# A one-core language-model tower: a new order of the first stage's turn, masked CB kept in PSUM, interleaved chains, and list scatters two at a time

## The reference, cut to what matters

```
h = quantised_rows(table)[x]                       # abs-max per row, round to 127 steps
# SSD block, per sequence of 128 tokens
zxbcdt = layernorm(h) @ in_proj.T
xBC    = silu(causal_conv_4_taps(xBC) + conv_b)    # x (384), B (128), C (128)
dt     = softplus(dt_raw + dt_bias)                # 6 heads
CB     = C @ B.T                                   # 128 x 128, lower triangle only
y      = (CB * exp(segsum(dt*A))) @ (x*dt) + D*x   # per head, 64 columns each
y      = rmsnorm(y * silu(z)) * norm_w
h      = h + layernorm(h) + sigmoid(gate) * (y @ out_proj.T)
# routing: two routers of 4 experts, top 1; common experts, and unique ones
# for tokens over a capacity of 2048 per common expert
h      = h + layernorm(h) + common(h) + dropped * unique(h)
```

## Time and profile before

| | us |
|---|---|
| three timed runs, median (lowest to highest) | 1097.21 (1094.24 to 1099.18) |
| the profiled execution, device time | 1107.01 |
| its span in the profile | 1105.2 |
| first stage, to the start of the last turn's first `mix` | 593.1 |
| 15 turns from the first `mix` to that one (t = 2 to 16) | 533.0 |

### The profile page before, as it was taken

The page is one execution under the profiler, slowest core; times in us unless marked ns, Lnnn a source line. Parts: engine busy times, 40 slices in busy tenths (PEclk is TensorE's granted clock), DMA queues, the critical chain, the costliest instruction groups (busy, mean ns, idle before and its releaser), DMA issues.

```text
span 1105.2 us, 18876 instructions
## 1 busy us (share of the span) xinstructions
PE 931.3 (84%) x5730; PEld 626.5 (57%) x5731; DVE 679.1 (61%) x2089; ACT 564.6 (51%) x1163; POOL 573.0 (52%) x751
## 2 busy tenths in 40 slices
PE   2688899888888889989888597999897977979986
PEld 2233455445554555545546475767675756768874
DVE  3687999898998989889887234777211211112111
ACT  3666886777767877588664224232232221323330
POOL 7332645456465655463434555234556656556543
PEclk9898998999999998899997788999888979889988
DMA  4910011001110111010001122133332111112211
GB/s 101 319 50 2 15 44 45 30 17 45 44 42 6 44 45 45 2 45 30 30 31 60 34 64 66 58 99 111 90 89 54 54 46 49 49 54 73 73 56 29
DMA packets 50179, 61.91 MB, mean 56 GB/s; under 512 B 22668, under 2 KB 41832, under 8 KB 49556
## 3 DMA queue, kind: packets, MB, share of 16 engines
q0 software_dynamic: 16704, 30.54, 9.8%
q1 hardware_dynamic: 28724, 24.91, 7.6%
q10 hardware_dynamic: 4640, 5.13, 1.5%
HBM read 36.22 MB, written 25.92 MB: 56 GB/s over the span
## 4 chain that ended last, share of the span: by engine, by line
PE 40%; DVE 24%; issue 13%; ACT 12%; another core or an unknown queue 5%; POOL 3%; DMA 2%; DVEq 1%; ACTq 0%; POOLq 0%
DVE xbc L1526 9%; PE yb L1304 5%; PE mm L1147 5%; PE cx L1304 5%; PE mm L1282 4%; PE mm L1275 4%; PE mm L1151 3%; PE sg L1275 3%; DVE mix L1546 2%; PE tp L1114 2%; PE sg L1065 2%; ACT rows_s L831 2%; DVE ybuf L1559 2%; DMA xg<-hr_dram,ids 1%
## 5 line engine op out<-in xcount | busy, mean ns | idle before, releaser
L1526 DVE SCALAR_TENSOR_TENSOR xbc<-mm,cw,xbc 128x508 f32<-128x508 f32 (+2 forms) x231 | 168.5, 741 | 27.5 <-ACT xbc L806 19.9
L1147 PE MATMUL mm<-xt_a,win_a 128*128 128x512 f32 x248 | 144.2, 666 | 38.0 <-DVE xbc L1526 28.8
L979 ACT ACTIVATE ht<-mm,b1s 128x256 f32<-128x256 f32 x102 | 44.8, 473 | 256.8 <-PE sg L1275 119.9
L689 POOL DMA_INDIRECT out_dram<-osb,ids_s x80 | 81.9, 1024 | 139.4 <-DVE osb L1900 122.9
L1900 DVE TENSOR_TENSOR osb<-cx,res 128x192 f32<-128x192 f32 x40 | 14.3, 357 | 180.0 <-remote 90.3
L806 ACT ACTIVATE xbc<-mm,cb,cw 128x512 f32<-128x512 f32 x77 | 56.5, 774 | 123.2 <-PE mm L1151 122.2
L549 POOL TENSOR_TENSOR ybuf<-ybuf,zs 128x384 f32<-128x384 f32 x64 | 69.3, 1084 | 73.7 <-DVE ybuf L1559 71.6
L670 POOL DMA_INDIRECT xg<-hr_dram,ids x80 | 80.4, 1005 | 47.6 <-issue 23.8
L1304 PE MATMUL yb<-w2s,ht 128*128 x408 | 85.1, 359 | 10.3 <-issue 10.2
L1304 PE MATMUL cx<-w2s,ht 128*128 x408 | 77.8, 337 | 14.9 <-issue 14.9
L1275 PE MATMUL mm<-fx_a,w1a_t 128*128 128x256 f32 x240 | 82.1, 426 | 9.6 <-issue 5.7
(11 more groups left out here) (304 smaller groups left out, 2101.1 us busy)
## 6 DMA issues: line engine op xcount, KB each, us to landing
hr_dram<-hr SPq DMA_DIRECT2D x16, 768.0 KB
w2s<-in_w2c_dram SPq DMA_DIRECT2D x4, 576.0 KB
w2s_u<-in_w2u_dram ACTq DMA_DIRECT2D x4, 576.0 KB
list_c<-fill SPq DMA_DIRECT2D x2, 1032.0 KB, 12.4
list_u<-fill SPq DMA_DIRECT2D x2, 1032.0 KB, 18.7
w1a<-in_w1c_dram SPq DMA_DIRECT2D x4, 384.0 KB
w1a_u<-in_w1u_dram ACTq DMA_DIRECT2D x4, 384.0 KB
xg<-hr_dram,ids POOLq DMA_INDIRECT x80
```

The costliest lines, as they stand in the source:

```text
L689: nc.gpsimd.indirect_dma_start(out=out_rows, out_offset=bass.IndirectOffsetOnAxis(ap=ids_s[:, v, t, 0:1], axis=0), in_=osb[:, v, t, :], in ...
L1147: mmul(tile_bank(g2, m)[:, :], win_a[:, column(m):column(m) + P], xt_a[:, p, :], start=True, stop=False)
L1526: ins = stt(out=dst_[:, :, back:L], in0=src[:, :, 0:L - back], scalar=cw[:, m, TAPS - 1 - back:TAPS - back], in1=dst_[:, :, back:L], op0=A ...
```

## The change

- **Order of the turn.** PE, ACT and DVE call the same functions in another order, which the diff shows in full. PE begins with cbx(0) and seg(0), ahead of project(0); seg(2) comes ahead of project(2); cbx(1) after project(2); side, cbx(2), y(1), side_back stand between project(3) and project(4). ACT does `sum_rows` right after the large Silu and ahead of start(6) and start(7). DVE does weights(1) after conv(1) and ahead of y(0), weights(2) ahead of quantise and y(1).
- **Masked CB in PSUM.** `cbm` is gone: DVE masks CB in place in `cx`, and `mix` reads it from there. The join stands behind `xd`. PE's `cbx` of sequence j+1 therefore waits for `mix` of sequence j instead of `xd`.
- **Interleaved chains.** `softplus` is cut into its instructions, and they stand between the taps of conv(4), the rows of residual(0) and the tiles of y(2). `pick` and `stats2` are interleaved with each other in even turns.
- **Counts.** `more` and `acc` are gone: the running count stands in a spare slot at either end of `oh`, and one reduction over the batch's slots and the running one makes the next.
- **POOL.** The four scatters in each of two places become two in each of four places; the gathers of group t+2 move from the middle of the turn to its end, behind `norm1`, and read their row numbers from `xids` without the copy into `gidx`.

```diff
@@ POOL body
                 list_tokens(0)
                 rms()
                 gate_y(1)
-                if t + 2 < NG:
-                    gather(t + 2)
                 route_x()
+                list_tokens(1)
                 route_y()
                 gate_y(2)
+                list_tokens(2)
                 norm2()
-                list_tokens(1)
+                route()
+                list_tokens(3)
                 gate_y(3)
                 if t + 1 < NG:
                     norm1(t + 1)
+                if t + 2 < NG:
+                    gather(t + 2)
@@ ACT body
                 decays(0)
                 start(0)
+                decays(1)
                 start(1)
-                decays(1)
+                decays(2)
                 normed2()
                 squares()
-
                 start(2)
                 start(3)
-                decays(2)
+                copy_side()
                 normed()
-                copy_side()
-
+                decays(3)
+                with_rest()
+                exp_steps()
                 start(4)
-                exp_steps()
+                exp_logits()
+                from_tp(0)
                 start(5)
-                exp_logits()
-                with_rest()
-                from_tp(0)
-                decays(3)
-                silus()
                 if t + 1 < NG:
                     rounded(t + 1)
-                from_tp(1)
+                silu_xbc()
+                sum_rows()
                 start(6)
                 start(7)
-                sum_rows()
+                silu_z()
+                from_tp(1)
@@ PE cbx and body
                     pe.wait_ge(s_xbc, g3 + 1)
-                    wait(pe, s_xd, GS * g3 + j)
+                    wait(pe, s_m, GS * g3 + j)
...
-                project(0)
                 cbx(0)
                 seg(0)
+                project(0)
                 project(1)
                 seg(1)
                 prefixes()
                 y(0)
+                seg(2)
+                project(2)
                 cbx(1)
-
-                project(2)
                 project(3)
-                seg(2)
+                side()
+                cbx(2)
                 y(1)
-                side()
-
+                side_back()
                 project(4)
-                cbx(2)
-                side_back()
+                seg(3)
                 project(5)
+                to_tp(0)
                 out_product(0)
-                to_tp(0)
-                seg(3)
+                cbx(3)
                 y(2)
-
+                to_tp(1)
                 project(6)
-                cbx(3)
                 out_product(1)
-                to_tp(1)
                 step_sums()
                 project(7)
                 y(3)
@@ DVE weights and places
-                    wait(dve, s_m, GS * g3 + j)
-                    link(tt(cbm[:, :], cx[:, 0:P], le[:, :], ALU.mult))
+                    link.go(tt(cx[:, 0:P], cx[:, 0:P], le[:, :], ALU.mult))
...
+                    link.join()
                     dve.wait_ge(s_e, GS * g3 + j + 1)
                     stt(out=mix[:, j % 2, :, :], in0=dec[:, j % 2, :, :], scalar=1.0,
-                        in1=cbm[:, :].unsqueeze(1).broadcast_to([P, HEADS, P]), op0=ALU.min, op1=ALU.mult).then_inc(s_m, 1)
+                        in1=cx[:, 0:P].unsqueeze(1).broadcast_to([P, HEADS, P]), op0=ALU.min, op1=ALU.mult).then_inc(s_m, 1)
...
-                    tt(acc[:, :], acc[:, :], more[:, :], ALU.add)
+                    v.tensor_reduce(running(b + 1), with_running(b, n), AX.X, ALU.add)
@@ DVE body
                 weights(0)
                 conv(0)
                 conv(1)
+                logits()
+                weights(1)
                 y(0)
                 places()
-
-                weights(1)
                 conv(2)
                 conv(3)
-                y(1)
+                side_read()
+                steps_abs()
+                weights(2)
                 if t + 1 < NG:
                     quantise(t + 1)
-                side_read()
-                steps_abs()
-                logits()
-
-                weights(2)
-                conv(4)
-                residual(0)
-                softplus()
-                y(2)
-
+                y(1)
+                conv(4, (soft_sum, soft_inverse))
+                soft_ratio()
+                residual(0, (0,))
+                soft_square()
+                residual(0, (1,))
+                soft_top()
+                y(2, (0,))
+                soft_term(3)
+                y(2, (1,))
+                soft_term(2)
+                y(2, (2,))
+                soft_term(1)
+                soft_term(0)
+                soft_steps()
+                soft_rates()
                 weights(3)
                 residual(1)
-                pick()
-                stats2()
+                rows_read()
+                pick((lambda: row_moments(0), lambda: row_moments(1), lambda: row_moments(2), lambda: row_moments(3),
+                      row_sums, row_shift))
                 y(3)
```

199 lines of the change are left out of this document (135 added, 64 removed).

## The result

The changed kernel takes 1068.65 us, the median of four runs (1064.87 to 1070.94); the kernel before took 1097.03 beside it. The ratio is 0.973, 95% interval 0.968 to 0.977. The change saves 28 us where 38 were forecast: inside the forecast's own band (1044 to 1074), at its slow end. The profiled execution took 1070.94 us, its span is 1069.2.

What follows compares the result with a forecast made beforehand. VectorE's stream (33.4 us a turn) bounds until TensorE stops it at 32.6 against 35.53: 44 us saved in fifteen turns, less 6 for clock and ramp, 38; median 1097.2 to 1059, forecast 1044 to 1074 (0.55).

Steps and rivals of the forecast that it cites:

- the clock: Fifteen first-stage turns: TensorE would have no room left at low granted clock; three such turns cost some 4 us more.
- The ramp: Start of kernel: group 2's gathers now stand behind norm1 of group 1 while weights load; priced 0 to 5, 2 taken.
- Chains: VectorE's linked instructions: each broken link worth 0.12 us; 1.56 us a turn plus 0.48 from `pick` and statistics, together 2.0.
- the term of the softplus: VectorE, taps of conv(4) and softplus: 12 linked neighbours, three remain, so 9 links go at 0.12 us each, every turn.
- The stalls: TensorE's side products: stalls no semaphore explains, 1.0 and 0.3 us in about every second turn, 0.65 a turn.
- VectorE's stream: VectorE's work with gaps, without waits, per turn: the bound at 33.4 us, falling by 3.1 to 30.3, below TensorE's 31.03.
- `mix`: VectorE: long cases come from both inputs in SBUF; CB in PSUM saves 0.67 us a turn, plain cost unchanged.
- TensorE: Per turn: 31.03 us busy, 0.65 stalls, 0.6 waits for taps, 0.3 for weights(1) and odd turns; 32.6 in all.
- The last turn: Last first-stage turn keeps its order, CB products wait for `mix`: 0 to 2 us against a little gain, taken as 0.
- The links are worth nothing: Rival: VectorE drains behind every instruction anyway; only 1.1 us a turn go, turn 34.0, 1076 us; chance 0.05.
- TensorE gives less: Rival: low clock in every second turn, or prefixes and tight weights(1), make turns 33.7 to 34.5, 1074 to 1091; chance 0.17.
- The gathers come late: Rival: VectorE waits for gathers issued at turn's end, margin 1.8 us in odd turns; slower 0.07, about as before 0.08.

Runs made afterwards that it cites:

- the first experiment: Kernel before with only the masked CB kept in PSUM, read there by `mix`, join behind `xd`: 1022.03 us against 1028.95, ratio 0.995, fast chip.
- the kernel with the tile behind: Changed kernel with y(2)'s third tile moved behind the softplus's last instructions (`dts`, rates), gathers at turn's end: 984.11 us, ratio 0.957 to the kernel before, fast chip.

## Why the prediction came out as it did

**The band was right, the point 10 us too fast.** Of the 11 us between the 38 forecast and the 27.4 of the first pair's first stage, 7.7 lie in the 15 turns (40 forecast, 44 less 4 for the clock, against 32.3) and 2.9 in the last turn. The ramp came out at the 2 us of its price, and the cause that was named is there, VectorE standing for the gathered rows:

```profile
47.00 0.95 DVE L1440 TENSOR_REDUCE q<-gath 128x4 f32<-128x768 f32 x1 [4.71 <-DMA gath<-in_table_dram,xids]
```

The price itself was met by luck. On the fast chip the gathers' place alone is worth 4.7 us of ramp; so something else in the change gives some 2.7 back, and the prediction had no such term.

**Chains: right in size, wrong in what they brought with them.** The links are worth what rows 4 and 5 said; the starts of the timeline after agree. The step that failed is the term of the softplus, 9 links at 0.12 us, taken as it stands. The same edit moves the third tile of y(2) ahead of the softplus's end, and so POOL's gate onto `dts`. The term that was missing is (12.6 - 3.2)/16 = 0.6 us a turn, 9 us in 15 turns by the busy times; removing it brought 0.56 to 0.61 us a turn on the fast chip, where the clock was full in both traces. On the slow chip it was not removed, so that it is behind the 7.7 us missing there is worked out, not shown. It could have been read before: `acc<-acc,more` in the earlier trace rows, 4 elements and 829 ns, was priced as something to get rid of, when it showed what can happen to any instruction with both inputs in SBUF behind a tile of y.

**The stalls, a rival on the slow chip.** They were priced from one turn, 1.3 us in every second one, 9.8 in all. The kernel before has 6.1 in its 15 turns, so this was too much for it; that the changed kernel has 9.9 meets the price by luck. And a stall costs more than its own length. Five turns with stalls, from 189.42 in every second turn, take 33.81 to 36.09 us, two of them at clock 0.95; on the fast chip, without stalls, the same five take 31.82 to 31.84. That is 15.2 us, as much as the 15 turns of the two traces differ (14.8), and 5.4 more than was priced. VectorE's wait for the side values behind the stalls (10.0 us, 3.3 before) is on the slow chip only. With the collision this makes 14 us of missing terms against 7.7 missing, so other terms were priced too high; no run on the slow chip parts them.

**VectorE's stream.** Forecast: 33.4 to 30.3, 3.1 us a turn. Measured, from the windows less the listed waits: before 35.53 - 36.3/15 = 33.1 (all seven rows of that view; the forecast used three), after 33.38 - 42.5/15 = 30.55. That is 2.55, and 0.6 are missing.

**`mix`.** The time was right, 72.0 to 60.4 us for 64, and the plain cost too. The cause that was named is half of it. PSUM does cure it (the first experiment), but the new order cures most of it without PSUM (63.3 with the order alone, 62.9 with everything but PSUM). The Trainium skill, VectorE: DVE Perf Modes, section on the TRN2 errata, would have made `mix` 65 ns longer with a PSUM source, by the prediction's estimate. The trace disagrees: 944 ns from PSUM, 948 from SBUF in the same order.

**Order.** The forecast gave the order no gain of its own beyond VectorE's 2.1 us of waits. Alone it saves 18.5 us, and the other two parts are worth 7 and 2 us without it. The step that took VectorE's stream for the bound, so that whatever the change frees on it counts, was too simple for the order of before: there the two other parts hardly count. That the waits at the turn's end take up their gain is argued from the waits for the decays, not shown by a run of its own.

**TensorE.** 31.31 busy and 2.07 idle were measured, 31.3 (with the clock) and 1.55 forecast. The waits of 0.7 and 0.5 ahead of project(2) and project(3) are 0.4 and 0.5; the wait for `rows_s` is gone, as forecast. On the fast chip the changed kernel's turn is 32.40, below the forecast 32.6, but without the stalls that the forecast had in it.

**The last turn.** Priced at 0, it cost 2.9. The window of before, then of after, then of the kernel with the tile behind and with the order alone (third column from the end: clock):

```profile
593.12:605.27 12.15, 12.15 (x106) 8.62 (x106) 7.47 (x21) 3.21 (x9) 7.57 (x7) 0.67 0.43 134
```

```profile
562.86:577.92 15.06, 14.16 (x104) 9.80 (x105) 7.31 (x21) 3.17 (x8) 6.55 (x7) 0.54 0.35 108
```

```profile
542.90:553.88 10.98, 9.89 (x103) 7.12 (x104) 7.22 (x21) 3.22 (x8) 6.53 (x7) 0.78 0.48 149
```

```profile
563.42:573.64 10.22, 9.91 (x104) 7.22 (x105) 7.54 (x21) 2.56 (x7) 6.30 (x7) 0.81 0.52 160
```

Length times clock is 8.1, 8.1, 8.6 and 8.3. TensorE is at the lower level (1.2 GHz) at the start of this turn in all four: the two matrix products of the first CB take 0.77 us, against 0.49 at 2.4 GHz. Ahead of it TensorE stood idle (it was busy 3.9 to 5.8 of the last 7 us), and this turn has no projections. It comes back to 2.4 GHz at a different point: the second CB takes 0.49 in the third and fourth kernel and still 0.80 in the first two. After the change the first CB product waits 0.90 us for `mix`, and TensorE's busy time rose by 2.0; these are the 2.9. The order does not set this by itself, since the kernel with PSUM alone, in the old order, has a last turn of 15.51. So the length of the last turn goes with the clock, 10.2 to 15.5 us, and the medians hold it; why the clock comes back early in some kernels stays open.

**Rivals.** *The links are worth nothing* falls: a turn at 34.0 was its result, and the trace shows the early starts. The Trainium skill, VectorE: DVE Perf Modes, section The DRAIN you can't avoid, says the semaphore costs nothing extra; the trace disagrees by 0.12 us at this length. *TensorE gives less* (33.7 to 34.5 a turn) came close on the slow chip at 33.4. (Its upper end was added up wrong: 34.5 a turn, less the 6 us taken off, is 1088 and not 1091.) *The gathers come late* fell: past the ramp VectorE never waits for them. What I named as proof against me, a turn of 34 or more at clock 1.00, is there twice (34.51 and 34.05); both turns hold stalls in the side products. A second such sign, a wait of the masks for CB of over 1.5 us in odd turns, is there twice too, 3.18 and 2.21 us, both in turns at clock 0.90: there TensorE is late with CB.

## What to carry to other kernels

Every instruction of VectorE with two inputs in SBUF is a possible victim of POOL, and the shortest ones lose most for their size. Some with one input are too, as the conversion of 8 numbers shows. After any reorder or interleaving ask which of them now stands just behind the instruction that releases POOL, and put that release behind them instead. Where two engines feed each other, a part that frees one of them may be worth little until the order lets it count; and an idle slot of half a microsecond can be the slack on which the other's next step rests. Compare turns of the same kind at the same clock before trusting a sum over all of them.
